# Self-attention in one column grouping: score tiles and transposes as four column groups of 32

## The chip, the cores and the metric

The kernel runs on one core of a Trainium2 chip. The metric is the device time of one execution in microseconds; three runs of the kernel before gave 1753.58, 1754.51 and 1754.3, median **1754.3**.

## What is computed

A decoder layer on x of 4 x 1024 x 256 in f32, with normalization after each part: an attention by autocorrelation, a cross-attention to 64 rows of context, and a feed-forward part that itself consists of a self-attention (16 heads of 16) and a mixture of 8 experts. The change touches that self-attention alone:

```
def _msa(x, w_qkv, w_proj):
    qkv = (x @ w_qkv).reshape(b, n, 3, H, DK)          # b=4, n=1024, H=16, DK=16
    attn = jnp.einsum('bhnd,bhmd->bhnm', q, k) * (1.0 / np.sqrt(DK))
    attn = jax.nn.softmax(attn, axis=-1)
    y = jnp.einsum('bhnm,bhmd->bhnd', attn, v)
```

## The kernel before, in words

The layer runs as stages one after the other, each with its own instruction stream per engine and semaphores between them. `self_attention` (L963) comes after the projection to q, k and v, and before `gate`.

It works through 64 heads (4 batches x 16). q and k of a head arrive from DRAM split into three bf16 parts each and are laid out as 96 rows (`R`), so that one bf16 matmul over 96 rows gives the score at nearly f32 accuracy; three more rows of q hold the row's maximum, and three of k hold -1, so that a matmul over 99 rows gives the score less its maximum.

TensorE (PE) has a software pipeline by hand. `slot(s)` (L1096) works on four heads at once, each further along than the next, and the order of its pieces is written out at L1179 to L1190:
- `a(k)`, L1105: for head s, the scores of 128 queries against 1024 keys, two matmuls of 512 columns into one of two pairs of banks. VectorE (DVE) takes each pair's row maximum (`top`, L1240).
- `maxima()`, L1158: the transpose of the 128 x 8 maxima of the head just finished. ScalarE (ACT) copies it, GpSimd splits it in three bf16 parts, and SyncE's queue writes them into q's rows 96 to 98.
- `b(m, h)`, L1121: for head s - 2, scores the other way round (128 keys against 512 queries, 99 rows), 16 of them into three rotating banks (`rotating`, L1004). ACT takes the exponential of each (L1206) into `pT`.
- `products(m0, lag)`, L1142: v (32 columns, one of them ones, for the sum) times `pT`, in f32. The 1024 queries are split in four parts of 256, and part j goes to PSUM partitions 32j to 32j + 31, so four matmuls occupy the four groups of 32 columns of the array. A call does two of the eight key tiles. Four calls a slot: L1180, L1183, L1187, L1189.
- `results()`, L1167: two transposes of `y_raw`, whose sums DVE inverts (L1249) and multiplies (L1251).

So a slot has 16 matmuls in `a`, 16 in `b`, 32 in `products` and 3 transposes. Scores and transposes use the array over all its 128 columns (the maxima 8 of them), the products over 32 each. Waits stand on the first instruction of a piece; `maxed`, `exped`, `mxT_read` and `y_stored` free the banks.

`slots` (L1007) runs s = 0 to 3 written out, then a loop of 15 rounds over a body of four slots (s = 4 to 63), then three slots that empty the pipeline. Each engine has its own such loop. An f32 matmul shows as two pairs of a weight load (LDWEIGHTS, engine PEld) and a matmul, a bf16 matmul and an f32 transpose as one pair.

Of the kernel before, what the change touches and what calls it, by code (L numbers as in the profile page):

```python
# [18 lines left out]
P = 128  # L19
TPB = S // P  # L20
# [942 lines left out]
def self_attention(nc, ctx, t, dram):  # L963

    def sb(name, shape, dt=F32):
        return ctx.enter_context(nc.sbuf_tensor("sb_m_" + name, shape, dt))

    def sem(name):
        return ctx.enter_context(nc.semaphore("m_" + name))

    ps, pz, ident, v_all, y_all = t["ps"], t["pz"], t["ident"], t["v_all"], t["y_all"]
    HEADS = B * H
    R = 6 * DK
    NB = 4
    q_s = sb("q", [R + 3, NB, S], BF16)
    k_s = sb("k", [R + 3, NB, S], BF16)
    v_s = sb("v", [P, 2, TPB, 32])  # L980
    pT = sb("pT", [P, TPB, S])
    mx = sb("mx", [P, 2, TPB])
    mxT = sb("mxT", [TPB, P])
    mx_rest = sb("mx_rest", [TPB, P])
    mx_parts = sb("mx_parts", [TPB, 2, 3, P], BF16)
    y_raw = sb("y_raw", [P, 256])
# [4 lines left out]
    set_up, v_in, scores1, maxed, mxT_done, mxT_read, split_done = (sem(n) for n in (  # L991
        "set_up", "v_in", "scores1", "maxed", "mxT_done", "mxT_read", "split_done"))
    y_rec, spare = sem("y_rec"), t["spare"]
    scores2, exped, pv, y_copied, yT_done, y_stored, pool_steps = (sem(n) for n in (
        "scores2", "exped", "pv", "y_copied", "yT_done", "y_stored", "pool_steps"))
# [8 lines left out]
    def rotating(use):  # L1004
        return 4 + ROTATION.index(use) % 3
# [11 lines left out]
    def has(s, lag, edge):  # L1017

        return edge is None or 0 <= s - lag < HEADS

    def turn(par, it, lag):

        return (par - lag) % NB, it + 1 - (1 if par < lag else 0)

    with nc.Block() as block:
        @block.sync
        def _(sp):
            def load(g, i):
                for dst, src, rows in ((q_s, "q_parts", ((0, 3), (0, 2), (0, 1))), (k_s, "k_parts", (0, 1, 2))):
                    at = 0  # L1030
                    for n, r in zip((3, 2, 1), rows):
                        for j in range(n):
                            part = (r[0] + j) if src == "q_parts" else r
                            sp.dma_start(dst[at:at + DK, i, :], dram[src][part, ds(g * DK, DK), :]).then_inc(q_in[i], 16)
                            at += DK

            load(0, 0)

            def slot(s, par, it, edge):
                if has(s, -1, edge):  # L1040

                    if not (edge == 0 and s + 1 < NB):
                        sp.wait_ge(scores2, W * (s + 2 - NB))
                    load(s + 1, (par + 1) % NB)
                if has(s, 1, edge):
                    i, _ = turn(par, it, 1)
                    sp.wait_ge(split_done, s)
                    for r in range(3):
                        sp.dma_start(q_s[R + r:R + r + 1, i, :].rearrange("o (t n) -> o t n", t=TPB),
                                     mx_parts[:, (par - 1) % 2, r, :]).then_inc(max_in[i], 16)  # L1050

            for s in range(NB):
                slot(s, s, 0, 0)
            with sp.Fori(1, HEADS // NB - 1) as it:
                for q in range(NB):
                    slot(it * NB + q, q, it, None)
            for s in range(HEADS - NB, HEADS + 3):
                slot(s, s % NB, s // NB, HEADS)
# [33 lines left out]
        @block.tensor  # L1092
        def _(pe):
            pe.wait_ge(set_up, 3)

            def slot(s, par, it, edge):  # L1096
                one, after, two, three = has(s, 0, edge), has(s, 1, edge), has(s, 2, edge), has(s, 3, edge)
                e = s - 2
                first = edge == 0 and s == 2
                if one:  # L1100
                    i, use = turn(par, it, 0)
                if two:
                    i2, use2 = turn(par, it, 2)

                def a(k):  # L1105
                    if not one:
                        return
                    if k == 0:
                        pe.wait_ge(q_in[i], 12 * 16 * use)
                    if not (edge == 0 and s == 0 and k < 2):  # L1110
                        pe.wait_ge(maxed, TPB * s + k - 1)
                    for h in range(2):
                        mm = pe.matmul(ps[2 * (k % 2) + h][:, :], q_s[0:R, i, k * P:(k + 1) * P],  # L1113
                                       k_s[0:R, i, h * 512:(h + 1) * 512], start=True, stop=True)
                    mm.then_inc(scores1, 1)


                FREE = {"b00": -2, "b01": -1, "b10": 0, "mxT": 1, "b11": 2, "b20": 3, "b30": 4, "b31": 5, "yT": 6,
                        "b40": 7, "b41": 8, "b51": 9, "b60": 10, "b61": 11, "b70": 12, "b71": 13}

                def b(m, h):  # L1121
                    if not two:
                        return
                    use = f"b{m}{h}"
                    if use == "b00":
                        pe.wait_ge(max_in[i2], 48 * use2)
                    if use == "b21" and after:
                        pe.wait_ge(mxT_read, s)
                    elif use == "b21":
                        pe.wait_ge(exped, W * e + 1)  # L1130
                    elif use == "b50" and three:
                        pe.wait_ge(y_stored, s - 2)
                    elif use == "b50":
                        pe.wait_ge(exped, W * e + 6)
                    elif not (first and FREE[use] <= 0):
                        pe.wait_ge(exped, W * e + FREE[use])
                    elif first and use == "b00":
                        pe.wait_ge(mxT_read, 1)
                    pe.matmul(ps[rotating(use)][:, :], k_s[:, i2, m * P:(m + 1) * P],  # L1139
                              q_s[:, i2, h * 512:(h + 1) * 512], start=True, stop=True).then_inc(scores2, 1)  # L1140

                def products(m0, lag):  # L1142
                    if not has(s, lag, edge):
                        return
                    g, par2 = s - lag, (par - lag) % 2
                    if m0 == 0:
                        if not first:
                            pe.wait_ge(y_copied, g)
                        pe.wait_ge(v_in, g + 1)
                    pe.wait_ge(exped, W * g + 2 * (m0 + 2))  # L1150
                    for m in range(m0, m0 + 2):
                        for j in range(4):
                            mm = pe.matmul(ps[7][32 * j:32 * j + 32, 0:256], v_s[:, par2, m, :],  # L1153
                                           pT[:, m, j * 256:(j + 1) * 256], start=(m == 0), stop=(m == TPB - 1),
                                           skip_group_check=True)
                    mm.then_inc(pv, 1)

                def maxima():  # L1158
                    if not after:
                        return  # L1160
                    pe.wait_ge(maxed, TPB * s)
                    if two:
                        pe.wait_ge(exped, W * e + FREE["mxT"])
                    pe.transpose(ps[rotating("mxT")][0:TPB, 0:P], mx[:, (par - 1) % 2, :],
                                 ident[:, :]).then_inc(mxT_done, 1)

                def results():  # L1167
                    if not three:
                        return
                    pe.wait_ge(y_copied, s - 2)  # L1170
                    if two:
                        pe.wait_ge(exped, W * e + FREE["yT"])
                    else:
                        pe.wait_ge(exped, W * HEADS)
                    for r in range(2):
                        tr = pe.transpose(ps[rotating("yT")][:, r * P:(r + 1) * P], y_raw[:, r * P:(r + 1) * P], ident[:, :])
                    tr.then_inc(yT_done, 1)

                a(0), b(0, 0), b(0, 1), a(1), b(1, 0)  # L1179
                products(6, 3)  # L1180
                maxima()
                b(1, 1), b(2, 0), a(2), a(3), b(2, 1), b(3, 0)
                products(0, 2)  # L1183
                b(3, 1)
                results()
                b(4, 0), a(4), a(5), b(4, 1), b(5, 0), b(5, 1)
                products(2, 2)  # L1187
                b(6, 0), a(6), b(6, 1), b(7, 0), a(7)
                products(4, 2)  # L1189
                b(7, 1)  # L1190

            slots(pe, slot)
# [776 lines left out]
```

## Time and profile before

| | |
|---|---|
| median of three runs | 1754.3 us |
| the profiled execution | 1753.78 us |
| its span, first to last instruction | 1751.8 us |
| self-attention (596 to 1322 us) | 726 us |
| PE busy in it | 721.8 us |
| granted clock of TensorE, mean of the span | 0.954 |

The span is cut into stages by time. PE is TensorE's matmuls and PEld its weight loads, which overlap them; DVE, ACT, POOL and SP are the others. A line number (L1153) is that of the kernel before. Rows with a start time list neighbouring instructions of one line as one entry with their count; the difference of two starts is what one of them keeps the engine for, while the duration of a matmul covers its whole way through the array and overlaps the next one's. Queue q8 carries instruction code.

### The profile page before, as it was taken

The numbers are of one execution on the slowest core, as the hardware profiler recorded it, in microseconds if no ns is written. First come the engines' busy times: TensorE is split into PE (matmuls) and PEld (weight loads), VectorE is DVE, ScalarE is ACT, GpSimd is POOL, SyncE is SP. The second block draws the span as 40 slices with busy tenths as digits, with TensorE's granted clock in tenths as the row PEclk, the third lists the DMA queues.
The fourth block names the chain that finished last, engine by engine and source line by source line (L and its number), as shares of the span: only waits on it lengthen the run. The fifth ranks groups of instructions, "written<-read, shape, count | busy, mean of one in ns | idle before, by whom it ended". The sixth has DMA issues, their size and how long they took to land. (4 is left out here: it accounts for less than half of the span.)

```text
span 1751.8 us, 35770 instructions
## 1 busy us (share of the span) xinstructions
PE 1596.5 (91%) x11156; PEld 909.1 (52%) x11157; DVE 1138.9 (65%) x1685; ACT 844.6 (48%) x1505; POOL 399.8 (23%) x670
## 2 busy tenths in 40 slices
PE   6997699996886999999999999999997839999997
PEld 3554356654452344444444444444436728898886
DVE  2545379997655788888888888888854752233322
ACT  1211144432442677777777777777783302221221
POOL 3110211100432111111111111111112314555553
PEclk9999599999997899999999999999998859999999
DMA  6000200000222111111111111111107435555552
GB/s 198 0 0 1 64 1 1 0 1 1 108 108 99 32 35 37 36 32 33 37 36 32 33 37 36 32 33 37 36 10 229 143 108 190 188 177 195 195 181 77
DMA packets 82275, 123.69 MB, mean 71 GB/s; under 512 B 24339, under 2 KB 48533, under 8 KB 82230
## 3 DMA queue, kind: packets, MB, share of 16 engines
q1 hardware_dynamic: 76614, 107.77, 20.2%
q0 software_dynamic: 5616, 15.34, 2.6%
q8 instruction: 26, 0.43, 0.1%
q14 instruction: 19, 0.16, 0.0%
HBM read 96.56 MB, written 26.08 MB: 70 GB/s over the span
## 5 line engine op out<-in xcount | busy, mean ns | idle before, releaser
L1240 DVE TENSOR_REDUCE sb_m_mx<-banks 128x1 f32<-128x1024 f32 x512 | 603.3, 1220 | 103.4 <-PE banks L1113 102.8
L1206 ACT ACTIVATE sb_m_pT<-banks 128x512 f32<-128x512 f32 x1024 | 552.2, 594 | 159.5 <-PE banks L1139 151.8
L1139 PE MATMUL banks<-sb_m_q,sb_m_k 99*128 99x512 bf16 x1024 | 329.6, 383 | 1.4 <-ACT sb_m_pT L1206 1.3
L1113 PE MATMUL banks<-sb_m_k,sb_m_q 96*128 96x512 bf16 x1024 | 293.3, 388 | 12.8 <-DMA sb_m_k<-k_parts 10.4
L1153 PE MATMUL banks<-sb_m_pT,sb_m_v 128*32 128x256 f32 x4096 | 275.0, 386 | 0.7 <-ACT sb_m_pT L1206 0.7
L1153 PEld LDWEIGHTS banks<-sb_m_pT,sb_m_v 128*32 128x32 f32 x4096 | 107.0, 109 | 152.6 <-issue 74.7
L1139 PEld LDWEIGHTS banks<-sb_m_q,sb_m_k 99*128 99x128 bf16 x1024 | 99.1, 97 | 162.1 <-ACT sb_m_pT L1206 84.4
L1113 PEld LDWEIGHTS banks<-sb_m_k,sb_m_q 96*128 96x128 bf16 x1024 | 98.9, 98 | 125.3 <-issue 15.0
L1084 POOL CAST sb_m_mx_parts<-sb_m_mxT 8x128 bf16<-8x128 f32 x64 | 18.2, 284 | 630.1 <-ACT sb_m_mxT L1219 608.5
L1785 ACT ACTIVATE sb_e_hT<-banks 128x512 f32<-128x512 f32 x78 | 46.6, 597 | 238.6 <-PE banks L1744 238.6
L1755 PE MATMUL banks<-w,sb_e_hT 128*128 x624 | 144.2, 384 | 8.7 <-ACT sb_e_hT L1785 5.1
L1744 PEld LDWEIGHTS banks<-sb_e_xT,w 128*128 128x128 f32 x1248 | 146.9, 194 | 4.3 <-DVE sb_e_xT L1795 1.3
L1744 PE MATMUL banks<-sb_e_xT,w 128*128 128x128 f32 x1248 | 147.4, 277 | 1.8 <-DVE sb_e_xT L1795 1.8
L1755 PEld LDWEIGHTS banks<-w,sb_e_hT 128*128 128x128 f32 x624 | 115.4, 190 | 29.8 <-issue 15.3
L1802 DVE TENSOR_TENSOR sb_e_x<-sb_e_x,banks 128x256 f32<-128x256 f32 x39 | 16.4, 421 | 123.4 <-PE banks L1755 119.9
L1795 DVE TENSOR_SCALAR sb_e_xT<-banks,table_ln_w,table_ln_b 128x128 f32<-128x128 f32 x78 | 28.4, 406 | 54.9 <-PE banks L1734 54.9
L705 ACT ACTIVATE sb_b_pr<-sb_b_pr 128x1024 f32<-128x1024 f32 x32 | 33.9, 1058 | 58.3 <-DVE sb_b_pr L742 57.5
L633 PE MATMUL banks<-sb_b_kblk,sb_b_qT 128*128 128x512 f32 (+1 forms) x128 | 60.2, 593 | 0.0
L884 PE MATMUL banks<-sb_c_xT,w_qkv 128*128 128x512 f32 x128 | 56.5, 597 | 3.5 <-ACT sb_c_xT L907 3.1
L181 PE MATMUL banks<-sb_w_qk,sb_xfT 128*128 128x512 f32 x128 | 56.8, 596 | 3.1 <-DMA sb_inv_even<-in_inv_even 3.1
L755 DVE RECIPROCAL sb_b_rec<-banks 128x256 f32<-128x256 f32 x32 | 56.0, 1752 | 2.4 <-PE banks L657 2.4
L644 PE MATMUL banks<-sb_b_w_o,sb_b_yT 128*128 128x256 f32 x128 | 35.3, 399 | 19.3 <-DVE sb_b_yT L758 19.3
(215 smaller groups left out, 1853.5 us busy)
## 6 DMA issues: line engine op xcount, KB each, us to landing
w<-in_w SPq DMA_DIRECT2D x47, 1024.0 KB, 11.9
sb_m_q<-q_parts SPq DMA_DIRECT2D x384, 32.0 KB, 1.7
sb_m_k<-k_parts SPq DMA_DIRECT2D x384, 32.0 KB, 1.7
q_parts<-sb_c_parts SPq DMA_DIRECT2D x24, 256.0 KB, 2.2
k_parts<-sb_c_parts SPq DMA_DIRECT2D x24, 256.0 KB, 2.2
X<-in_x SPq DMA_DIRECT2D x4, 1024.0 KB, 10.9
z_rows<-sb_g_zs SPq DMA_DIRECT2D x8, 512.0 KB, 3.4
x_rows<-X SPq DMA_DIRECT2D x8, 512.0 KB, 4.7
```

Source lines behind the costliest of these rows:

```text
L181: mm = pe.matmul(ps[4 + f % 4][:, :], xfT[:, k, r, q * P:(q + 1) * P], w_qk[:, k, :], start=(k == 0), stop=(k == KT - 1 and f != 3))
L633: mm = pe.matmul(ps[2 * (r % 2) + c][:, :], qT[:, c, r // GT, r % GT * P:(r % GT + 1) * P], kblk[:, c, ds(b, 1), :].rearrange("p o n -> p ...
L755: dve.reciprocal(rec[:, :], ps[6][:, D:2 * D]).then_inc(rec_done, 1)
L884: mm = pe.matmul(ps[4 + 2 * (u % 2) + h][:, :], w[:, k, u * P:(u + 1) * P], xT[:, k, h * 512:(h + 1) * 512], start=(k == 0), stop=(k == KT ...
L1113: mm = pe.matmul(ps[2 * (k % 2) + h][:, :], q_s[0:R, i, k * P:(k + 1) * P], k_s[0:R, i, h * 512:(h + 1) * 512], start=True, stop=True)
L1139: pe.matmul(ps[rotating(use)][:, :], k_s[:, i2, m * P:(m + 1) * P], q_s[:, i2, h * 512:(h + 1) * 512], start=True, stop=True).then_inc(sco ...
L1153: mm = pe.matmul(ps[7][32 * j:32 * j + 32, 0:256], v_s[:, par2, m, :], pT[:, m, j * 256:(j + 1) * 256], start=(m == 0), stop=(m == TPB - 1 ...
L1206: act.activation(pT[:, m, h * 512:(h + 1) * 512], ps[rotating(f"b{m}{h}")][:, :], ACT.Exp).then_inc(exped, 1)
L1240: dve.tensor_reduce(mx[:, par % 2, k:k + 1], pz[:, 2 * (k % 2):2 * (k % 2) + 2, :].rearrange("p q n -> p (q n)"), AX.X, ALU.max).then_inc( ...
L1744: mm = pe.matmul(ps[2 * q + m // 4][:, m % 4 * P:(m % 4 + 1) * P], w1[:, q, k, m * P:(m + 1) * P], xT[:, q, k, :], start=(k == 0), stop=(k ...
L1755: mm = pe.matmul(ps[6][:, 0:D], hT[:, q, m, :], w2[:, ds(e, 1), m, :].rearrange("p o n -> p (o n)"), start=(m == 0), stop=(m == HT - 1))
L1785: act.activation(hT[:, q, 4 * h:4 * h + 4, :], ps[2 * q + h][:, :].rearrange("p (m n) -> p m n", m=4), ACT.Gelu_apprx_tanh).then_inc(h_cop ...
```

## The change

Every matmul of the stage now writes 32 partitions of PSUM. A score matmul becomes four, each with 32 of the 128 stationary columns, all with the same 512 moving columns; the first carries the wait, the last the signal. The transpose of the maxima becomes a matmul with the identity as moving operand. The two transposes of the results become eight such matmuls. Data, banks, waits and the other engines stay.

```
                     for h in range(2):
-                        mm = pe.matmul(ps[2 * (k % 2) + h][:, :], q_s[0:R, i, k * P:(k + 1) * P],
-                                       k_s[0:R, i, h * 512:(h + 1) * 512], start=True, stop=True)
+                        for c in range(0, P, 32):
+                            mm = pe.matmul(ps[2 * (k % 2) + h][c:c + 32, :], q_s[0:R, i, k * P + c:k * P + c + 32],
+                                           k_s[0:R, i, h * 512:(h + 1) * 512], start=True, stop=True)
                     mm.then_inc(scores1, 1)
...
-                    pe.matmul(ps[rotating(use)][:, :], k_s[:, i2, m * P:(m + 1) * P],
-                              q_s[:, i2, h * 512:(h + 1) * 512], start=True, stop=True).then_inc(scores2, 1)
+                    for c in range(0, P, 32):
+                        mm = pe.matmul(ps[rotating(use)][c:c + 32, :], k_s[:, i2, m * P + c:m * P + c + 32],
+                                       q_s[:, i2, h * 512:(h + 1) * 512], start=True, stop=True)
+                    mm.then_inc(scores2, 1)
...
-                    pe.transpose(ps[rotating("mxT")][0:TPB, 0:P], mx[:, (par - 1) % 2, :],
-                                 ident[:, :]).then_inc(mxT_done, 1)
+                    pe.matmul(ps[rotating("mxT")][0:TPB, 0:P], mx[:, (par - 1) % 2, :],
+                              ident[:, :], start=True, stop=True).then_inc(mxT_done, 1)
...
                     for r in range(2):
-                        tr = pe.transpose(ps[rotating("yT")][:, r * P:(r + 1) * P], y_raw[:, r * P:(r + 1) * P], ident[:, :])
+                        for c in range(0, P, 32):
+                            tr = pe.matmul(ps[rotating("yT")][c:c + 32, r * P:(r + 1) * P],
+                                           y_raw[:, r * P + c:r * P + c + 32], ident[:, :], start=True, stop=True,
+                                           skip_group_check=True)
                     tr.then_inc(yT_done, 1)
```

## Rows read from the trace of the kernel before

**Rows 1.** The page: busy us of each engine; weight loads of the products, mean ns

```profile
PE 1596.5 (91%) x11156; PEld 909.1 (52%) x11157; DVE 1138.9 (65%) x1685; ACT 844.6 (48%) x1505; POOL 399.8 (23%) x670
...
L1153 PEld LDWEIGHTS banks<-sb_m_pT,sb_m_v 128*32 128x32 f32 x4096 | 107.0, 109 | 152.6 <-issue 74.7
```

**Rows 2.** Windows: stretch, length, busy of PE, PEld, DVE, ACT, POOL; clock; DMA

```profile
596.00:1322.00 726.00, 721.81 (x6144) 295.29 (x6142) 599.05 (x608) 564.47 (x1121) 100.23 (x305) 1.00 0.14 33
...
650.00:1297.00 647.00, 647.00 (x5485) 265.69 (x5479) 549.78 (x556) 502.50 (x998) 90.39 (x275) 1.00 0.14 34
```

**Rows 3.** Waits from 700 to 1290 us: total us, times, longest us

```profile
ACT sb_m_pT L1206 <- PE banks L1139: 113.3, 256, 0.9
DVE sb_m_mx L1240 <- PE banks L1113: 78.2, 152, 0.8
```

**Rows 4.** Line L1164, 700 to 1290 us: count, ns min/median/max, first and last start

```profile
L1164 PE MATMUL banks<-ident_sb,sb_m_mx x51: 272/273/273, 705.6 to 1289.4; 128*8 128x128 f32 x51
```

**Rows 5.** Timeline of PE in steady slots: start us, us, line, count

```profile
1000.68 0.38 PE L1176 MATMUL banks<-ident_sb,sb_m_y_raw 128*128 128x128 f32 x2
1000.90 0.38 PE L1139 MATMUL banks<-sb_m_q,sb_m_k 99*128 99x512 bf16 x1
1001.12 1.03 PE L1113 MATMUL banks<-sb_m_k,sb_m_q 96*128 96x512 bf16 x4
1001.99 0.81 PE L1139 MATMUL banks<-sb_m_q,sb_m_k 99*128 99x512 bf16 x3
...
1004.83 0.59 PE L1113 MATMUL banks<-sb_m_k,sb_m_q 96*128 96x512 bf16 x2
1005.35 1.07 PE L1153 MATMUL banks<-sb_m_pT,sb_m_v 128*32 128x256 f32 x16
1006.36 0.39 PE L1139 MATMUL banks<-sb_m_q,sb_m_k 99*128 99x512 bf16 x1
...
1009.19 0.27 PE L1164 MATMUL banks<-ident_sb,sb_m_mx 128*8 128x128 f32 x1
1009.30 0.60 PE L1139 MATMUL banks<-sb_m_q,sb_m_k 99*128 99x512 bf16 x2
```

**Rows 6.** Timeline of PE in cross-attention, from 265.0 to 267.5 us

```profile
264.80 1.03 PE L644 MATMUL banks<-sb_b_w_o,sb_b_yT 128*128 128x256 f32 x4
265.76 0.64 PE L657 MATMUL banks<-sb_b_prT,sb_b_v_cur 128*32 128x128 f32 x16
266.22 0.62 PE L657 MATMUL banks<-sb_b_prT,sb_b_ones_pair 128*32 128x128 f32 x16
266.77 0.98 PE L625 MATMUL banks<-ident_sb,sb_b_pr 128*128 128x128 f32 x7
```

**Rows 7.** PE's sequencer by line, around 1022 us and at the loop's jump

```profile
L1150 PEldq EVENT_SEMAPHORE  x1: 51/51/51, 1022.2 to 1022.2; - x1
...
L1136 PEldq ALU_OP  x1: 32/32/32, 1022.8 to 1022.8; - x1
...
L1011 PEldq COMPARE_BRANCH  x1: 208/208/208, 1017.3 to 1017.3; - x1
```

**Rows 8.** DMA: whole span; 590 to 645; 650 to 1297; 311 to 366; 626 to 629

```profile
q8 instruction: 26, 0.43, 0.1%
...
q8 instruction: 4, 0.07, 0.5%
...
q14 instruction: 1, 0.01, 0.0%
...
DMA packets 0, 0.00 MB, mean 0 GB/s; under 512 B 0, under 2 KB 0, under 8 KB 0
...
q8 instruction: 1, 0.02, 2.0%
```

**Rows 9.** DMA issues of the whole span: us from issue to landing

```profile
sb_m_q<-q_parts SPq DMA_DIRECT2D x384, 32.0 KB, 1.7
...
sb_e_x<-x_rows,sb_e_numbers POOLq DMA_INDIRECT x39, 3.9
```

## The prediction

> **What bounds the kernel now.** I first read the page: PE is busy 91% of the span, DVE 65%, ACT 48% [rows 1]. The windows by stage place that: self-attention fills 726 us, 41% of the span, PE busy 721.8 of them at granted clock 1.00, while DVE has 599 and ACT 564; inside the steady loop PE is busy 647.00 of 647 us [rows 2]. Since ends of matmuls are modelled, a busy PE proves little, so I asked who waits. In 590 us of the loop ACT waits for PE 113 us and DVE 78 us [rows 3]; no wait of PE's matmuls stands in that view. The 51 maxima transposes start from 705.6 to 1289.4 us, so a slot (one head) takes 583.8/50 = **11.68 us** [rows 4]. The loop's 647 us are 55.4 slots, so DVE is busy 549.78/55.4 = 9.9 us a slot and ACT 502.50/55.4 = 9.1 [rows 2]. PE's instruction stream is the bound, DVE is next, 1.8 us behind.
>
> Now the starts on PE. Score matmuls follow each other at 0.87/4 = 0.217 us [rows 5]. A burst of products is four rounds through the four column groups (2 key tiles x 2 passes of f32). Between L1113 at 1004.83 (two of them) and the burst at 1005.35 lie 0.52 us where two pitches are 0.43, so 0.09 is extra; from the burst's start to L1139 at 1006.36 it is 1.01 us, where four rounds of 0.217 are 0.87, so 0.14 is extra [rows 5]. Four bursts then cost 4 x 0.23 = **0.92 us a slot** beyond their streaming. The sum closes: 32 x 0.217 + 4 x (1.01 + 0.09) + 0.11 (maxima, 1009.19 to 1009.30) + 0.22 (results, 1000.68 to 1000.90) = 6.94 + 4.40 + 0.33 = 11.67 us [rows 5].
>
> Is it the change of column grouping that costs, and not the change from bf16 to f32? Transposes in f32 stand between bf16 scores at 0.22 and 0.11 apart, with nothing extra [rows 5]. In cross-attention both neighbours are f32: L644 starts four matmuls at 264.80, L657 (32 columns) follows at 265.76, that is 0.96 for 4 x 0.217 = 0.87, again 0.09 extra [rows 6]. So grouping it is. After the change nothing in the stage but the first entry and the last exit regroups.
>
> **The change part by part.** *Score matmuls*: each becomes four instructions on four column groups with the same 512 moving columns. No row shows bf16 groups or four groups that read the same moving data. Nearest row: the products, whose 16 matmuls in four rounds take 1.01 us with the regrouping in it [rows 5]. Low bound 0.217 us for four, high bound four in sequence, 0.87. I take 0.217: in that time a pass of f32 moves 256 x 4 B per partition and column group, a bf16 group 512 x 2 B, the same; and weight loads of 0.11 us [rows 1] hide under it. Scores stay 6.94 us a slot.
>
> *Products*: unchanged, 16 rounds x 0.217 = 3.47 us, the 0.92 gone.
>
> *Transposes as f32 matmuls*: a transpose is one pass, an f32 matmul two. Rounds of 128 columns: L657's first 16 take 0.46 us, 0.11 a round with a little entry cost [rows 6]. Maxima: 2 x 0.11 = 0.22 (was 0.11). Results: 2 x 2 x 0.11 = 0.44 (was 0.22). Plus 0.33 us. They come later by as much for ACT (mxT) and DVE (reciprocal); both engines have over 1 us a slot to spare, so nothing more.
>
> *Waits*: only the first of four carries the old wait and only the last the old signal; nobody gets a new wait, no DMA moves. PE slot: 6.94 + 3.47 + 0.22 + 0.44 = **11.07 us**, 0.61 less, and still above DVE's 9.9. Some 62 steady slots give 38 us; the three tail slots hold 9 bursts (2.1 us, partly hidden by waits for ACT), so 39 in all, against the profiled execution's 1753.8 (span 1751.8; the median is 0.5 higher): **1714.8** on the scale of the median, if nothing else happens.
>
> *Instructions*: matmuls plus weight loads. A slot now issues 64 for scores, 128 for products, 6 for transposes = 198, as the rows count (10,964 in 55.4 slots [rows 2]). It becomes 256 + 128 + 4 + 32 = 420. The sequencer: it passed the wait ahead of a burst at 1022.2 and the register step behind its 32 instructions at 1022.8 [rows 7], at most 0.02 us each, and that was with a full queue. 420 x 0.02 = 8.4 us and some 25 register steps at up to 0.1 make 10.9: just under 11.07 at this upper bound. I charge nothing.
>
> *Code*: this is where I expect trouble. Queue q8 fetches code in blocks of 0.43 MB/26 = 16 KB [rows 8]. Counted from the source, TensorE's program has some 6,700 instructions, so 64 bytes each, and each block is fetched once. The first round of the loop over four slots drew 4 packets (590 to 645 us) without PE ever idling, so blocks are fetched ahead of need; from 650 to 1297 us not one came, so the 57 KB body (894 instructions: 4 x 198 and 102 register, wait and branch steps) stays in a store [rows 8]. Cross-attention's 57 KB body stayed too: none from 311 to 366 us, a whole pass [rows 8]. The new body is 4 x 420 + 102 = 1,782 instructions, **114 KB**: eight blocks unless it starts on a block's edge, and a ninth fetched ahead at its end. That is twice anything shown to stay. If it doesn't stay, the blocks inside the body are fetched ahead and hidden (a block lasts 256 x 0.026 = 6.7 us), but the jump back goes to a block that is gone, 14 times. Price of one: a block takes 2.0% x 16 engines x 3 us = 0.96 us [rows 8]; a small load needs 1.7 us from issue to landing, up to 3.9 for indirect ones [rows 9]. So 1.7 + 1.0 = 2.7 to 3.9. To it comes the restart, some 0.4 (the branch alone takes 0.21 [rows 7], as much again goes to the first weights), and from it goes what PE has queued, some 0.7 (three to four groups, an estimate from the lead in rows 7): 2.4 to 3.6, taken as 3.1 us. 14 x 3.1 = 43 us: 1714.8 + 43 = **1758**. Ends: 14 x 2 = 28 (1743) and 14 x 4 = 56 (1771); the low end of the whole cost is 0, if the body stays.
>
> The Trainium skill (Advanced Engine Details and Errata, ISA Cache) gives TensorE 128 KB in lines of 16 KB. By that, eight blocks fit and nine do not, which speaks for the refetch. It also says that there are only two lines, which rows 8 contradict; no row here shows more than six blocks staying.
>
> **The rivals.**
> - *A, forecast: mode cost gone, code refetched each round.* 1758, range 1743 to 1771. For it: the doubled body. Against: nothing shows the store's end.
> - *B: the code stays.* 1715 (1711 to 1720). For it: two bodies of 57 KB stayed without a trace of strain. Against: untested size.
> - *C, clearly slower: the groups of four come slower than 0.217.* Its place is every score group, 32 a slot, and it turns the change into a loss from 0.61/32 = 0.019 us a group even if the code stays. Price by the burst's own rate with its regrouping (1.01 us for 32 instructions, 0.0316 each): 420 x 0.0316 = 13.3 us a slot, (13.3 - 11.68) x 63 = +102 us, 1855. With no overlap at all, 32 x 0.65 = 20.8 us a slot, over 3000. Against it: L657 puts through 64 instructions in 1.01 us, 0.016 each [rows 6], though from a filled queue. The Trainium skill (TensorE: Matmul & The Clock Gate, "Wait - 56ns, not 53.3ns?") knows a decoding by firmware of 62 ns a matmul; by it the slot's 210 matmuls would take 13.0 us, but starts 0.01 us apart in a burst don't look like it.
> - *D: it doesn't do what it says.* The gaps stay (regrouping by data type or by weight shape after all), and the longer transposes remain: +0.33 x 62 = +20, 1775, or 1818 with the refetch. Against it: L644 to L657.
>
> **How the numbers follow.** A 0.50, B 0.30, C 0.14, D 0.06. A is the likeliest: 1758. The range reaches over B and A, 1712 to 1772, and leaves out C, D and A's edges (A alone: 1743 to 1771). A measurement of this kernel can tell 0.2%, 3.5 us. A splits around 1754.3 by its stall: under 2.6 us a jump (0.10) faster, about 2.6 to 3.1 (0.16) same, above (0.24) slower. Faster 0.10 + 0.30 = 0.40; same 0.16 + 0.01 = 0.17; slower 0.24 + 0.13 + 0.06 = 0.43.
>
> **What the profile would show.** Right: starts of score groups 0.217 apart, no extra before or after bursts, a slot of 11.07 us, PE idle 2 to 4 us once every four slots with packets on q8 at that time, over 10 more of them than 35 in all. B: no packet between the loop's second round and its end. C: spaced score groups all through the slot, ACT and DVE waiting longer for PE. D: the 0.09 and 0.14 still there. I am wrong in size if the stall at the jump is hidden by PE's queue, and wrong in kind if DVE, busy 9.9 us, needs over 11 with its hand-overs.

## The result and the profile after

The changed kernel takes 1795.4 us (median of 4 runs, 1794.2 to 1799.1) against 1754.4 of the kernel before: 1.0236 times as long, 95% interval 1.0220 to 1.0252. That is 41 us slower, and 37 us above the 1758 forecast, outside the range of 1712 to 1772.

The page of the changed kernel, PE's busy time and the queue that fetches code; they answer to the first line of [rows 1] and to [rows 8]:

```profile
PE 1589.2 (89%) x18260; PEld 1065.9 (59%) x18261; DVE 1140.0 (64%) x1685; ACT 853.1 (48%) x1505; POOL 400.2 (22%) x670
...
q8 instruction: 159, 2.61, 0.7%
```

PE is busy less than before, though it issues 7,104 matmuls more, and the code queue moved 159 blocks where it had moved 26. Who waits, from 700 to 1340 us (total us, times, longest us), against [rows 3]:

```profile
ACT sb_m_pT L1213 <- PE banks L1142: 133.3, 228, 4.9
DVE sb_m_mx L1247 <- PE banks L1115: 115.5, 124, 4.7
PEld banks L1115 <- issue: 55.4, 44, 4.4
PE banks L1115 <- issue: 41.5, 12, 4.0
```

The last line has no counterpart in the kernel before. PE stands twelve times for up to 4.0 us at L1115, the first score tile of a round, and waits for nothing that the profile shows. ACT and DVE, whose longest wait for PE had been 0.9 us, now wait up to 4.9 us behind it. The timeline of PE tells both halves of the story (start us, us, line, count, idle before); first a steady stretch, to be laid beside [rows 5], then a jump:

```profile
1002.04 1.00 PE L1142 MATMUL banks<-sb_m_q,sb_m_k 99*32 99x512 bf16 x12
1002.69 1.22 PE L1157 MATMUL banks<-sb_m_pT,sb_m_v 128*32 128x256 f32 x16
1003.56 0.57 PE L1142 MATMUL banks<-sb_m_q,sb_m_k 99*32 99x512 bf16 x4
1003.78 0.79 PE L1115 MATMUL banks<-sb_m_k,sb_m_q 96*32 96x512 bf16 x8
...
890.91 0.57 PE L1142 MATMUL banks<-sb_m_q,sb_m_k 99*32 99x512 bf16 x4
894.70 1.04 PE L1115 MATMUL banks<-sb_m_k,sb_m_q 96*32 96x512 bf16 x8 [3.21 <-issue]
895.52 1.07 PE L1142 MATMUL banks<-sb_m_q,sb_m_k 99*32 99x512 bf16 x8
```

Twelve grouped matmuls take 0.65 us, which is 3 x 0.217. The burst of products takes 0.87 us to the next start, which is 4 x 0.217, with nothing extra ahead of it and nothing behind. So the change does what it says. At 890.91 the last group of a round starts, and behind it PE stands 3.21 us. Behind the stall eight matmuls take 0.82 us, where at 0.217 us for four they take 0.43.

The branch at the end of TensorE's loop (duration in ns, lowest, median, highest), which had been 208 ns in [rows 7]:

```profile
L1012 PEldq COMPARE_BRANCH  x14: 4238/4685/5144, 638.4 to 1286.2; - x14
```

The windows of the changed kernel (stretch, length, busy PE, PEld, DVE, ACT, POOL, granted clock, DMA). The first line is the whole stage; the next four run from the start of one back jump to that of the next; the last five are cut around two stalls:

```profile
596.00:1362.00 766.00, 712.88 (x12922) 446.80 (x12914) 596.69 (x607) 571.75 (x1118) 100.54 (x305) 0.96 0.14 34
689.26:740.15 50.89, 47.23 (x845) 29.25 (x841) 39.71 (x41) 37.00 (x73) 6.61 (x20) 0.93 0.15 34
890.03:939.31 49.28, 46.06 (x845) 28.90 (x841) 39.71 (x41) 36.77 (x73) 6.60 (x20) 0.97 0.15 36
1038.26:1085.86 47.60, 44.40 (x845) 28.83 (x841) 39.61 (x41) 36.66 (x73) 6.59 (x20) 1.00 0.16 37
1085.86:1133.55 47.69, 44.41 (x845) 28.89 (x841) 39.62 (x41) 36.66 (x73) 6.59 (x20) 1.00 0.16 37
...
891.50:894.60 3.10, 0.00 (x0) 0.00 (x0) 0.45 (x1) 0.60 (x1) 0.00 (x0) 1.00 0.15 31
894.68:898.06 3.38, 3.36 (x32) 1.34 (x36) 1.79 (x2) 1.22 (x3) 0.00 (x0) 0.50 0.24 49
898.20:903.00 4.80, 4.80 (x105) 2.87 (x100) 3.25 (x5) 3.77 (x9) 1.64 (x5) 1.00 0.14 31
1087.50:1090.50 3.00, 0.00 (x0) 0.00 (x0) 0.28 (x1) 0.47 (x1) 0.00 (x0) 1.00 0.12 26
1090.60:1094.00 3.40, 3.40 (x65) 2.06 (x69) 2.35 (x2) 2.35 (x6) 0.09 (x1) 1.00 0.24 57
```

This is the view that explains the number. A round of four slots comes in three lengths, and the granted clock sorts them: 47.6 to 47.7 us where it is 1.00 all round, 49.2 to 49.8 where its mean is 0.97, 50.8 to 51.0 where it is 0.93. After the stall at 891 the clock is 0.50, the lower level of 1.2 GHz, from 894.67 on for 3.4 us: 32 matmuls went through in a stretch in which 65 do after the stall at 1087, where it stayed at 1.00.

### The profile page after: what moved, and what is told of

It reads as the page before. It is cut to its first block and busy times, and to the rows that moved or that the text cites. A ratio compares the mean times of both kernels' runs of the same rounds, so it can differ in the third digit from the quotient of the medians.

```text
span 1792.2 us, 49978 instructions
## 1 busy us (share of the span) xinstructions
PE 1589.2 (89%) x18260; PEld 1065.9 (59%) x18261; DVE 1140.0 (64%) x1685; ACT 853.1 (48%) x1505; POOL 400.2 (22%) x670
## 5 line engine op out<-in xcount | busy, mean ns | idle before, releaser
L1213 ACT ACTIVATE sb_m_pT<-banks 128x512 f32<-128x512 f32 x1024 | 559.1, 595 | 186.4 <-PE banks L1142 168.1
L1142 PE MATMUL banks<-sb_m_q,sb_m_k 99*32 99x512 bf16 x4096 | 463.6, 392 | 0.8 <-ACT sb_m_pT L1213 0.5
L1115 PE MATMUL banks<-sb_m_k,sb_m_q 96*32 96x512 bf16 x4096 | 369.5, 399 | 62.1 <-issue 49.1
L1157 PE MATMUL banks<-sb_m_pT,sb_m_v 128*32 128x256 f32 x4096 | 316.6, 388 | 0.7 <-ACT sb_m_pT L1213 0.7
L1115 PEld LDWEIGHTS banks<-sb_m_k,sb_m_q 96*32 96x32 bf16 x4096 | 150.6, 99 | 162.1 <-issue 80.0
L1142 PEld LDWEIGHTS banks<-sb_m_q,sb_m_k 99*32 99x32 bf16 x4096 | 186.5, 98 | 86.8 <-issue 8.7
L1157 PEld LDWEIGHTS banks<-sb_m_pT,sb_m_v 128*32 128x32 f32 x4096 | 167.8, 112 | 77.2 <-issue 7.4
L1181 PE MATMUL banks<-ident_sb,sb_m_y_raw 128*32 128x128 f32 x1024 | 52.1, 277 | 0.5 <-ACT sb_m_y_raw L1221 0.5
```

Of the source, the lines that this page charges most:

```text
L1115: mm = pe.matmul(ps[2 * (k % 2) + h][c:c + 32, :], q_s[0:R, i, k * P + c:k * P + c + 32], k_s[0:R, i, h * 512:(h + 1) * 512], start=True, ...
L1142: mm = pe.matmul(ps[rotating(use)][c:c + 32, :], k_s[:, i2, m * P + c:m * P + c + 32], q_s[:, i2, h * 512:(h + 1) * 512], start=True, stop ...
L1181: tr = pe.matmul(ps[rotating("yT")][c:c + 32, r * P:(r + 1) * P], y_raw[:, r * P + c:r * P + c + 32], ident[:, :], start=True, stop=True, ...
L1213: act.activation(pT[:, m, h * 512:(h + 1) * 512], ps[rotating(f"b{m}{h}")][:, :], ACT.Exp).then_inc(exped, 1)
```

## The experiments

From the result I had two theories. **Theory 1**: the grouped slots are as fast as forecast, and the whole loss sits in the 14 jumps back. **Theory 2**: the groups, or the longer code as such, hurt wherever they run. By theory 1 a jump costs (1795.4 - 1714.8)/14 = 5.8 us.

### No jumps at all

```diff
-            slots(pe, slot)
+            for s in range(HEADS + 3):
+                slot(s, s % NB, s // NB, 0 if s < NB else None if s < HEADS else HEADS)
```

> The changed kernel with TensorE's fifteen rounds of four slots written out one behind the other, so that its 14 jumps back are gone (its register arithmetic goes with them, since the waits are then on constants). Theory 1, the jumps: the changed kernel is 1795.4 us where the grouped slots alone would give 1714.8, so the 14 jumps cost 80.6 us, 5.8 each: 4.2 to 5.1 us of branch with the code fetched again, and the rest a clock of 0.5 for 3.4 to 6.8 us after each. Without them 1715 us (1711 to 1719), no slot over 12 us between 650 and 1297, the granted clock 1.0 throughout. Theory 2, the groups themselves bring the clock down or the long code starves the engine wherever it runs: then the time stays at 1795 (1785 to 1800).

Measured: 1717.0 us, 0.9782 of the kernel before (0.9766 to 0.9798). From 700 to 1250 us the queue still fetched 82 blocks, so the long code was read, and PE never stood for it (the code queue from 700 to 1250 us, then the window):

```profile
q8 instruction: 82, 1.34, 1.0%
...
650.00:1250.00 600.00, 599.28 (x11376) 395.32 (x11372) 536.50 (x542) 496.59 (x976) 88.97 (x270) 1.00 0.16 38
```

PE is busy 599.28 of 600 us at clock 1.00. Code that runs straight on is fetched ahead and costs nothing; the jump costs. Theory 2 falls.

### Long code without groups

```diff
-            slots(pe, slot)
+            for s in range(NB):
+                slot(s, s, 0, 0)
+            with pe.Fori(0, (HEADS // NB - 1) // 2) as it:
+                for q in range(2 * NB):
+                    slot(it * (2 * NB) + q + NB, q % NB, it * 2 + 1 + q // NB, None)
+            for s in range(HEADS - NB, HEADS + 3):
+                slot(s, s % NB, s // NB, None if s < HEADS else HEADS)
```

> The kernel before, ungrouped, with eight slots in TensorE's loop body in place of four (7 rounds of 8 and the last four slots written out): code of about the changed kernel's length, 7 jumps, no groups. Theory 1, the length of the body alone does it: 7 jumps at 5.8 us, +40 us, 1795 us (1782 if only the stall of 3.9 us counts and the clock does not fall); the instruction queue shows about 9 packets in each round. Theory 2, it takes the groups: 1754 us, as before.

Measured: 1799.5 us, 1.0257 (1.0239 to 1.0274), as slow as the changed kernel without one grouped score. Two rounds of eight slots and the six taken jumps:

```profile
691.89:793.21 101.32, 97.56 (x796) 39.12 (x792) 79.46 (x81) 72.94 (x145) 13.17 (x40) 0.95 0.14 33
994.86:1094.67 99.81, 96.48 (x796) 38.85 (x792) 79.47 (x81) 72.93 (x145) 13.18 (x40) 0.97 0.14 34
...
L1194 PEldq COMPARE_BRANCH  x6: 3294/3598/3888, 691.9 to 1194.2; - x6
```

Eight ungrouped slots should take 8 x 11.68 = 93.4 us; these two rounds take 7.9 and 6.4 more. There are six taken jumps and not the seven that I had counted, so one costs 45/6 = 7.5 us here, more than the 5.8. The branch itself is shorter than in the changed kernel, but the stretch of half clock is up to 10.2 us long, and behind each of the six stalls PE stands a second time, 0.9 to 1.7 us, until DVE has read its maxima. The length of the loop's body is enough; the price of a jump is not a constant.

### A hint ahead of the jump

```diff
-            slots(pe, slot)
+            for s in range(NB):
+                slot(s, s, 0, 0)
+            with nc.Fori(1, HEADS // NB, engines=OrderedEngineSet([mybir.EngineType.PE]), hint_back_edge=True) as it:
+                for q in range(NB):
+                    slot(it * NB + q, q, it, None)
+            for s in range(HEADS, HEADS + 3):
+                slot(s, s % NB, s // NB, HEADS)
```

> The changed kernel with a prefetch hint for the back jump as the first instruction of each of TensorE's rounds; nothing else is changed. Theory 1: if the hint brings the loop's head in before the jump, the branch falls from 4.2 to 5.1 us to under 1 us, the clock stays at 1.0 and the time is 1715 to 1722 us. If the hinted block is thrown out again before the jump, or the fetch behind the first block is as late as before, it stays at 1795. Theory 2 (the groups, not the jump): 1795.

Measured: 1717.0 us, 0.9780 (0.9764 to 0.9797). The hint is one instruction at the head of a round that names the coming jump. The branches are at 0.22 us (the lowest is the last one, not taken), and from 636 to 1262 us not one block was fetched by the queue q8:

```profile
L1202 PEldq COMPARE_BRANCH  x15: 80/216/239, 641.0 to 1260.5; - x15
```

That is more than I had expected of it: I had thought that the head would be fetched early, and instead it had never left.

### Where the blocks begin

```diff
+            with nc.Fori(1, HEADS // NB, engines=OrderedEngineSet([mybir.EngineType.PE]), head_slot={mybir.EngineType.PE: 0}) as it:
...
+            with nc.Fori(1, HEADS // NB, engines=OrderedEngineSet([mybir.EngineType.PE]), head_slot={mybir.EngineType.PE: 128}) as it:
...
+            with nc.Fori(1, HEADS // NB, engines=OrderedEngineSet([mybir.EngineType.PE]), head_slot={mybir.EngineType.PE: 128}, hint_back_edge=True) as it:
```

These are the loop lines of e4, e5 and e6, in this order; the lines around them are those of e3.

> The changed kernel with the first instruction of TensorE's loop placed at the start of a 16 KB block of code; nothing else is changed. The body of 1,782 instructions of 64 bytes (6.96 blocks) then lies in 7 blocks where it now touches 8. Theory 1, with a store of 8 blocks of which one is filled ahead of the running one: 7 and 1 fit, nothing is fetched again, the branch is at 0.2 us and the time is 1715 us (1711 to 1720). If the store is smaller than that, or what is run ahead past the jump throws a block out, the round still fetches 7 to 8 blocks and the time is 1795.

> The same placing as in e4, but with the first instruction of TensorE's loop in the middle of a 16 KB block; the same instructions, no hint. The body of 6.96 blocks then touches 8. Theory 1, a store of 8 blocks with one filled ahead: 8 and 1 don't fit, about 9 packets on the instruction queue in each round, the branch at 4.2 to 5.1 us, the time 1795 us (1790 to 1800). Theory 2, e4 was fast for another reason than where its blocks begin (the branch into the loop, a head fetched by another path): 1716 us.

> e5 with the prefetch hint as the first instruction of each round. In e3 the hinted kernel fetched nothing at all between 636 and 1262 us. Theory 1, the hint has the block ahead of the last one be the loop's head, which is already there, in place of the next block of the code, so 8 blocks are enough: no packets between 650 and 1250 us, 1717 us (1713 to 1722). Theory 2, e3 was fast because the hint had shifted the loop by an instruction or the loader had moved it: then with the head held in the middle of a block it is 1795 us.

The slot named is the place, counted in instructions within a block of 256, at which the loop's first instruction is put. Measured: e4 1716.3 us (0.9783, 0.9767 to 0.9799), e5 1793.1 (1.0222, 1.0198 to 1.0246), e6 1717.7 (0.9792, 0.9773 to 0.9812). e4 and e5 have the same instructions and differ only in the place of the first one. The branches of e4 and one of its rounds:

```profile
L1202 PEldq COMPARE_BRANCH  x15: 76/208/225, 638.3 to 1258.0; - x15
...
727.05:771.31 44.26, 44.26 (x845) 29.16 (x841) 39.62 (x41) 36.69 (x73) 6.59 (x20) 1.00 0.16 36
```

and of e5 two rounds, the blocks fetched from 700 to 1250 us, and the branches that lie from 650 to 1280 us:

```profile
741.85:792.95 51.10, 47.66 (x845) 29.51 (x841) 39.70 (x41) 37.02 (x73) 6.60 (x20) 0.93 0.15 34
1036.99:1083.91 46.92, 44.44 (x845) 29.50 (x841) 39.62 (x41) 36.67 (x73) 6.60 (x20) 1.00 0.16 37
...
q8 instruction: 101, 1.65, 1.4%
...
L1202 PEldq COMPARE_BRANCH  x12: 3657/4504/4737, 690.9 to 1234.7; - x12
```

101 blocks in 550 us, at 49.4 us a round, are nine in each. The body is 6.96 blocks long, and the nine show that one block more than it touches is fetched. From a block's edge it touches 7 and with one fetched ahead fills 8: nothing is fetched. From the middle of a block it touches 8, the ninth is fetched ahead, and with it all nine in every round. So TensorE's store holds eight blocks of 16 KB, 128 KB, in this kernel. The Trainium skill (Advanced Engine Details and Errata, ISA Cache) gives 128 KB for TensorE in lines of 16 KB: e4 and e5 agree with both. Its "Only 2 cache lines!" does not fit: e4 goes round its seven blocks fourteen times, from 640 to 1258 us, without one fetch. With the hint the eight blocks of e6 stay as well. The reading that fits e3 and e6 is that the block ahead of the last one is then the loop's head, which is there already, in place of a ninth; the traces show that nothing is fetched, not why.

### A body that no store of eight blocks can hold, with the hint

```diff
-            slots(pe, slot)
+            for s in range(NB):
+                slot(s, s, 0, 0)
+            with nc.Fori(0, (HEADS // NB - 1) // 2, engines=OrderedEngineSet([mybir.EngineType.PE]),
+                         hint_back_edge=True) as it:
+                for q in range(2 * NB):
+                    slot(it * (2 * NB) + q + NB, q % NB, it * 2 + 1 + q // NB, None)
+            for s in range(HEADS - NB, HEADS + 3):
+                slot(s, s % NB, s // NB, None if s < HEADS else HEADS)
```

> The changed kernel with eight slots in the body (some 3,560 instructions, 14 blocks, 7 jumps) and the hint. No store of 8 blocks holds this, so the loop's head has to be fetched in every round. Theory 1, the hint brings the head in before the jump: 7 branches at under 1 us, 1717 us (1713 to 1724), with some 14 packets in each round. Theory 2, the hint only saves the ninth block: 7 branches at 4.2 to 5.1 us and the clock's fall behind them, +40 us on 1716, 1757 us (1750 to 1762).

Measured: 1734.6 us, 0.9901 (0.9877 to 0.9924), between the two. Two rounds of eight slots (88.5 us without a stall) and the branches, whose lowest is the last one, not taken:

```profile
776.39:866.79 90.40, 88.66 (x1685) 58.03 (x1681) 79.23 (x81) 73.33 (x145) 13.19 (x40) 1.00 0.17 38
957.28:1049.94 92.66, 90.49 (x1685) 58.24 (x1681) 79.42 (x81) 73.43 (x145) 13.20 (x40) 0.98 0.16 37
...
L1202 PEldq COMPARE_BRANCH  x7: 88/2935/3267, 683.8 to 1232.9; - x7
```

The branch takes 2.9 us where it took 4.7 in the changed kernel, PE stands 1.7 to 2.2 us where it stood 3.1 to 4.0, and at three of the six stalls the clock falls to half. Six jumps cost 18 us, 3 each. Neither theory gave this. The fetch is not hidden; how much of the gain is the hint's isn't shown, for the same eight slots were not run without it, and e2's branches, unhinted, are at 3.3 to 3.9 us.

The code queue shows a part of the answer. These are its blocks while one branch lasts: two in the changed kernel (889.9 to 894.5 us, branch of 4393 ns), one at the odd jump of e5 (1036.9 to 1041.0 us, 3657 ns) and one in e7 (957.2 to 960.3 us, 2975 ns):

```profile
q8 instruction: 2, 0.03, 3.9%
...
q8 instruction: 1, 0.02, 1.9%
...
q8 instruction: 1, 0.02, 2.5%
```

Where the block ahead of the body's end is fetched at the time of the jump, it and the loop's head are under way together, and the branch takes 4.2 to 5.1 us (14 jumps of the changed kernel, 13 of e5). Where it has come before, only the loop's head is fetched: 3.3 to 3.9 us (the six of e2 and the one odd jump of e5). So one block at a time explains a good part of e7's gain over the changed kernel, and the hint at most the rest. No run varied this alone, and what the rest of the branch is made of stays open.

### Does standing idle alone bring the clock down?

Three tries at a stall of the same length in the kernel before, whose short code is never fetched again. The first two stand at the head of each round of TensorE's loop, with STALL = 80: e8, and e11 with a register addition in its place.

```diff
+                for _ in range(STALL):
+                    pe.nop(nofuse=True)
...
+                for _ in range(STALL):
+                    pe.reg_add(pad, pad, 1)
```

> The kernel before (ungrouped, short code, nothing fetched again) with 80 empty instructions at the head of each of TensorE's 15 rounds: at about 0.05 to 0.06 us each 4 to 5 us in which the engine gets no matmul, as long as the branch of the changed kernel, without a fetch of code. Theory 1, an idle stretch of that length is by itself what brings the granted clock to 0.5: it falls after each of the 15 stalls as in the changed kernel, and each costs the stall and 1.5 to 2.5 us more: 15 x 5.8 = +87 us, 1841 us (1825 to 1850). Theory 2, the clock's fall belongs to the fetch or to the grouped slots: the clock stays at 1.0 between 650 and 1297 and each stall costs only its own 3.9 us: +58 us, 1813 us (1800 to 1820).

> What e8 was to show: its 80 empty instructions took no time and left no record. Here 80 register additions stand at the head of each of TensorE's 15 rounds in the kernel before (at 0.056 us each 4.5 us; the code stays short and nothing is fetched again). TensorE then stands about 3.6 us in each round, as long as the 3.1 to 4.0 us of the changed kernel. In the changed kernel a round is 44.24 us and 3.4 for the stall, and 1.7 or 3.4 more where the granted clock was 0.5 for 3.41 or 6.83 us. Theory 1, standing idle that long brings the clock down by itself: it falls after most of the stalls, rounds of 46.71 + 3.6 + 1.7 to 3.4 = 52.0 to 53.7 us, 1833 to 1859 us in all. Theory 2, the fall belongs to the fetching of code: no 0.5 between 650 and 1297, rounds of 50.3 us, 1808 us.

Measured: e8 1755.5 us, 1.0009 (0.9999 to 1.0019), and e11 1755.1, 1.0002 (0.9992 to 1.0011). Both are inconclusive: the added instructions left no record, the rounds kept their 46.71 us, and PE never stood. They say nothing on the clock, and not what such an instruction costs either: whether the 80 reached the engine at all isn't shown. The third try, e12, is a wait at the head of TensorE's round (the first two lines) for an operation at the end of ScalarE's fourth slot:

```diff
+                if par == 0 and edge is None:
+                    pe.wait_ge(go, it)
...
+                if par == NB - 1 and edge != HEADS:
+                    act.activation(idle[:, :, :], ident[:, :].unsqueeze(1).broadcast_to([P, IDLE, P]),
+                                   ACT.Identity).then_inc(go, 1)
```

> The register additions of e11 left no record either. Here a real wait: in the kernel before, ScalarE ends every fourth slot with one more operation (128x3072 elements into a tile that nothing reads; by its 594 ns for 128x512 and 1058 ns for 128x1024 about 2.9 us), and TensorE's next round waits for it. TensorE stands the last exponential's 0.6 us, these 2.9 and the signals' way, 3.7 to 3.9 us in each of 15 rounds, with short code and nothing fetched. Theory 1, standing idle that long is by itself what brings the granted clock down: it falls to 0.5 for 3.41 or 6.83 us after most of the stalls, rounds of 46.71 + 3.8 + 1.7 to 3.4 = 52.2 to 53.9 us, 1836 to 1862 us in all. Theory 2, the fall belongs to fetching code or to the groups: the clock stays at 1.0 between 650 and 1350, rounds of 50.5 us, 1811 us.

Measured: 1846.7 us, 1.0517 (1.0499 to 1.0534). Two of its rounds, a stretch behind a stall, and that stall:

```profile
653.22:705.25 52.03, 48.50 (x400) 19.52 (x396) 39.77 (x41) 39.10 (x74) 6.58 (x20) 0.97 0.14 31
705.25:758.75 53.50, 49.97 (x400) 19.87 (x396) 39.78 (x41) 39.36 (x74) 6.58 (x20) 0.94 0.13 30
711.00:716.00 5.00, 5.00 (x25) 1.53 (x24) 2.45 (x2) 2.56 (x6) 0.18 (x1) 0.50 0.13 30
...
709.95 1.03 PE L1118 MATMUL banks<-sb_m_k,sb_m_q 96*128 96x512 bf16 x2 [3.53 <-ACT sb_m_idle L1230]
```

Every one of the 15 stalls is 3.5 us long, and with every one of them the granted clock falls to 0.50: rounds of 46.71 + 3.53 + 1.8 = 52.0, or of 53.3 to 53.7 us where it is down for longer. No code is fetched and no score is grouped. So standing idle is enough for the fall, and theory 2 of this run is out. In the changed kernel 12 of 14 stalls of 3.06 to 3.97 us had it, in e5 10 of 14 of 2.48 to 3.56 us, in e7 3 of 6 of 1.74 to 2.22 us. So at 3 us and more it is likely, not certain, and length alone doesn't decide: the stall of 3.06 us had it, one of 3.56 did not.

### The two halves of the edit

Both with the loop at a block's edge, so that no jump clouds them. e9 has groups for the scores only:

```diff
-                    pe.matmul(ps[rotating("mxT")][0:TPB, 0:P], mx[:, (par - 1) % 2, :],
-                              ident[:, :], start=True, stop=True).then_inc(mxT_done, 1)
+                    pe.transpose(ps[rotating("mxT")][0:TPB, 0:P], mx[:, (par - 1) % 2, :],
+                                 ident[:, :]).then_inc(mxT_done, 1)
...
-                        for c in range(0, P, 32):
-                            tr = pe.matmul(ps[rotating("yT")][c:c + 32, r * P:(r + 1) * P],
-                                           y_raw[:, r * P + c:r * P + c + 32], ident[:, :], start=True, stop=True,
-                                           skip_group_check=True)
+                        tr = pe.transpose(ps[rotating("yT")][:, r * P:(r + 1) * P], y_raw[:, r * P:(r + 1) * P], ident[:, :])
```

> e4 (the changed kernel with TensorE's loop at the start of a block, 1716.3 us, rounds of 44.24 us) with the three transposes of a slot left as whole transposes, so that only the score tiles are in groups. Theory 1, every whole operation between grouped ones costs about what a burst of products between whole scores costs in the kernel before, 0.09 + 0.14 = 0.23 us: the slot is 11.06 less the 0.33 us of the transposes' matmuls, and two places at 0.23 more, 11.19 us, 44.8 a round, 1724 us. Theory 2, a whole transpose changes nothing for the array: 10.73 us, 42.9 a round, 1695 us, and the transposes' edit is a loss in the change.

e10 is the opposite: the kernel before with only the transposes edited as in the change.

> The kernel before with its scores whole, and only the transposes made into matmuls (the results' in groups), its loop at the start of a block. It has both edits' other half. Theory 1: 11.68 + 0.33 for the matmuls and 0.23 for the results' groups standing between whole scores, 12.24 us a slot, 49.0 a round, 1790 us. Theory 2, where the transposes themselves had cost a switch in the kernel before, a part of it comes back: 11.8 to 12.0 us a slot, 1762 to 1775 us.

Measured: e9 1727.5 us, 0.9844 (0.9828 to 0.9861); e10 1793.6 us, 1.0215 (1.0198 to 1.0232). A round of e9 and, from its timeline, the results' transposes between grouped work:

```profile
866.62:911.39 44.77, 44.77 (x788) 21.58 (x784) 39.48 (x41) 37.04 (x73) 6.58 (x20) 1.00 0.15 36
...
883.50 1.04 PE L1158 MATMUL banks<-sb_m_pT,sb_m_v 128*32 128x256 f32 x16
884.36 0.39 PE L1143 MATMUL banks<-sb_m_q,sb_m_k 99*32 99x512 bf16 x4
884.69 0.44 PE L1181 MATMUL banks<-ident_sb,sb_m_y_raw 128*128 128x128 f32 x2
885.05 0.40 PE L1143 MATMUL banks<-sb_m_q,sb_m_k 99*32 99x512 bf16 x4
```

From the burst to the group behind it 0.86 us, nothing extra. From that group to the whole transposes 0.33 where 0.22 would do, from them back to groups 0.36 where 0.22 would do: 0.25 us for this place, close to the 0.23 of [rows 5]. At the transpose of the maxima it is 0.19: the burst at 880.59 keeps PE 0.97 us where 0.87 would do, and L1169 at 881.56 is followed after 0.20 where 0.11 would do. The two places cost 0.44 us where the forecast had 0.46. A slot is 44.77/4 = 11.19 us, as theory 1 forecast it, against 11.06 with the transposes in groups too. e10's rounds of 48.9 us are 12.23 a slot, with 12.24 expected. Each half alone is the poorer: the transposes' edit costs 0.55 a slot where the scores are whole and gains 0.13 where they are grouped.

## Why the prediction was wrong

**The bound and its terms: right.** PE's stream was the bound, the 0.92 us of regrouping went, the transposes' matmuls cost 0.33. The slot was forecast at 11.07 us; e4's round gives 44.26/4 = 11.06. The kernel without jumps was forecast at 1714.8 and measures 1716.3 to 1717.7 in four forms (e1, e3, e4, e6); 0.5 of the 1.5 us and more between is the step from the profiled execution to the median, which the sum names and leaves out. DVE did not take over.

**Charging nothing for issue: right.** e1 keeps PE at 599.28 of 600 us with 420 instructions a slot, and e4's round at 44.26 of 44.26 with the register steps besides. The Trainium skill (TensorE: Matmul & The Clock Gate, "Wait — 56ns, not 53.3ns?") gives about 62 ns for each matmul's decoding in firmware, for the case that the decoding in hardware is switched off; the prediction left that condition out. The estimate by that figure is 210 x 0.062 = 13.0 us a slot, and the measured slot of 11.06 us is shorter, so no such cost bounds this kernel.

**Choosing A over B: right in kind.** The body did not stay, nine blocks were fetched in every round, and PE stood once in four slots. It was a close call for a reason that the prediction named in passing: eight blocks "unless it starts on a block's edge". e4 is that case, and B with it.

**The price of a jump: the step that failed.** "14 x 3.1 = 43 us" has two faults, and the trace of the changed kernel separates them against the undisturbed 44.24 us of a round:

- *What the stall does to the clock* was no term of the sum. Twelve of the fourteen stalls brought the lower clock, seven for 6.83 us and five for 3.41, 64.9 us in all. Of these, 8.0 us lie within the stalls, where the fall came up to 1.9 us before PE started again and cost nothing. The other 56.9 us are work at half speed, which gives up half of that, 28 us.
- *The stall itself* was taken too short. PE stands 3.06 to 3.97 us, 49.1 us in the 14 jumps, 3.51 each. In the two rounds without a fall the whole loss is 3.36 and 3.45 us where PE stands 3.20 and 3.28, so 0.16 more goes with each. That makes 3.67 us a jump and 51 us in all, 8 more than the 43.

The first of these falls, seen from inside the stall that ends at 643.81 us:

```profile
642.10:643.70 1.60, 0.00 (x0) 0.00 (x0) 0.00 (x0) 0.00 (x0) 0.00 (x0) 0.50 0.15 42
```

The 14 rounds from 638.39 to 1337.13 us take 698.7 us, 14 x 44.24 is 619.4, so the jumps cost 79.4; the two parts give 51 + 28 = 79. The distance to the forecast is closed within 1 us: 1758 + 1.5 (the base) + 8 + 28 = 1795.5, measured 1795.4. That idling is enough for the clock's fall is shown by e12.

That the stall came out within 0.6 us of the forecast is in part luck, for its terms were off in opposite directions. The fetch and the restart were to take 2.7 to 3.9 and 0.4 us; the branch lasts 4.24 to 5.14 us, and the next matmul starts 0.27 us behind it. The work that PE still had when the branch began was put at 0.7 us; it lasted 1.45 us at every one of the 14 jumps.

The trace of before could have told. Where self-attention ends, at 1320.4 us, PE stands for 2.0 us after a stretch in which it was already less busy, and from 1321.3 us on, within that stand, the granted clock is 0.50 for 10.2 us. These are the windows of the kernel before ahead of that place and from inside the gap on:

```profile
1300.00:1320.00 20.00, 17.69 (x179) 6.46 (x172) 1.00 (x4) 17.08 (x35) 1.63 (x5) 1.00 0.01 1
1321.40:1331.50 10.10, 7.65 (x21) 6.11 (x22) 0.69 (x1) 2.88 (x3) 0.00 (x0) 0.50 0.40 80
```

I had read the granted clock as 1.00 in [rows 2] and taken it along into a loop with idle stretches that the loop of before did not have. The range had the same hole: its upper end allowed 4 us a jump and had nothing behind the stall.

**The rivals.** B (1715) is what the kernel does as soon as its loop fits. C is ruled out by starts at 0.217 and D by the missing gaps.

**The better kernel.** e3, e4 and e1 take 2.2% less time than the kernel before and 4.4% less than the changed one, and they do not differ from each other. e3 needs one argument and no placing, but its body must fit as well: with 14 blocks (e7) the stall is back. e4 depends on a body of at most seven blocks.

## What to carry over

An edit that multiplies instructions inside a loop has a price at the loop's end: count the body in blocks of code, its start within a block and the block fetched ahead included, and hint the back jump or place the head before giving up the edit. When a sum contains an idle stretch of TensorE of some 2 to 4 us, look in the same trace for what the granted clock does in and after such a stretch, and carry it as a term of its own; here it was more than half of the stall's own price again. And judge edits that remove a switch together: each of the two halves here is worth less alone, and one is a loss.

## What the runs showed of the hardware

- TensorE's code stayed when it filled eight blocks of 16 KB with the one fetched ahead (e4) and was fetched anew, all nine, when it needed a ninth (e5: 101 blocks in 550 us, and not just the one that was too many).
- A taken back jump to code that is gone lasted 4.2 to 5.1 us in the changed kernel, where two blocks were fetched at the jump; 3.3 to 3.9 in e2, with one; 2.8 to 3.3 in e7, with one and the hint. One to code that is there 0.21, and 0.22 with the hint.
- When TensorE stood idle, the granted clock often went from 1.0 to 0.5, within the idle stretch or up to 1.7 us after it: at 15 of 15 stretches of 3.52 to 3.53 us (e12), 12 of 14 of 3.06 to 3.97 us (the changed kernel), 10 of 14 of 2.48 to 3.56 us (e5) and 3 of 6 of 1.74 to 2.22 us (e7). After those at 1039.7 and 1087.3 us of the changed kernel it stayed at 1.00.
- A change between whole and grouped operation cost 0.23 us there and back around products; around the transposes of e9 it was 0.25 and 0.19.
- Groups of four bf16 matmuls that read the same moving 512 columns started 0.217 us apart for the four, as fast as one whole matmul.
- 80 empty instructions, and 80 register additions whose result nobody reads, left no record and took no time (e8, e11). The delay that worked (e12) was built from an operation that the engine waits for.
